# Convolution filters kept as (high, low) pairs instead of two separate rows

## What is computed

```python
x = x + L0(gn(x))     # mixture of 8 experts, top 2: silu(x w1) * (x w3), then w2
x = x + L1(gn(x))     # three causal depthwise convolutions (3, 7, 15 taps), then a 96 -> 32 mix per head
x = x + L2(gn(x))     # the same with other weights
x = x + L3(gn(x))     # the same with other weights
```

## Time and profile before

| | |
|---|---|
| median of three runs | 1167.75 us (1167.03 to 1170.06) |
| the profiled execution | 1165.23 us, span 1163.6 us |
| mean granted TensorE clock | 0.957 |
| TensorE matmuls busy | 1058.7 us, 91% |
| weight loads busy | 881.7 us, 76% (beside matmuls) |
| VectorE, ScalarE, GpSimd busy | 494.9, 318.1, 138.7 us |

### The profile page before, as it was taken

One profiled execution on the slowest core, in us unless ns is written; L12 is line 12 of the kernel. 1 busy time (PEld: TensorE's weight loads), 2 busy tenths in 40 slices (PEclk: granted clock), 3 DMA queues, 4 the chain that ended last, 5 costly groups with the idle time before them and its releaser, 6 DMA issues. The chain is left out here.

```text
span 1163.6 us, 14424 instructions
## 1 busy us (share of the span) xinstructions
PE 1058.7 (91%) x5266; PEld 881.7 (76%) x5267; DVE 494.9 (43%) x677; ACT 318.1 (27%) x433; POOL 138.7 (12%) x170
## 2 busy tenths in 40 slices
PE   5579999999999999999999999357999979999998
PEld 2377887887887887887877878247888967888887
DVE  5744245244245163245362452045424862378011
ACT  2402143243143153143341431112301220122112
POOL 2002121220221221221122211100000000000000
PEclk9769999999999999999999999768999989999999
DMA  9236216415613718316419132293998299688993
GB/s 361 82 116 231 36 28 236 145 27 186 204 26 130 252 27 288 102 27 224 157 28 352 27 128 36 67 265 76 212 185 183 48 219 215 142 173 188 202 208 100
DMA packets 66336, 172.72 MB, mean 148 GB/s; under 512 B 8192, under 2 KB 38016, under 8 KB 57280
## 3 DMA queue, kind: packets, MB, share of 16 engines
q1 hardware_dynamic: 58080, 149.19, 45.1%
q0 software_dynamic: 8080, 23.07, 9.4%
q10 hardware_dynamic: 144, 0.02, 0.0%
HBM read 136.15 MB, written 40.30 MB: 152 GB/s over the span
## 5 line engine op out<-in xcount | busy, mean ns | idle before, releaser
L1345 PE MATMUL head_ps<-split,ring 128*128 128x512 f32 (+1 forms) x630 | 223.9, 355 | 15.6 <-DMA ring<-filters 13.9
L1349 PE MATMUL head_ps<-split,ring 128*128 128x512 f32 (+1 forms) x630 | 218.4, 347 | 0.0
L1346 PE MATMUL head_ps<-split,ring 128*128 128x512 f32 (+1 forms) x630 | 218.2, 346 | 0.0
L1345 PEld LDWEIGHTS head_ps<-split,ring 128*128 128x128 f32 x630 | 121.7, 193 | 32.0 <-DMA ring<-filters 14.5
L1349 PEld LDWEIGHTS head_ps<-split,ring 128*128 128x128 f32 x630 | 121.6, 193 | 15.9 <-DVE split L1163 0.2
L1346 PEld LDWEIGHTS head_ps<-split,ring 128*128 128x128 f32 x630 | 121.9, 194 | 14.8
L860 PE MATMUL y_ps<-w_hi,hT_hi 128*128 128x512 f32 x280 | 115.9, 414 | 1.2 <-ACT hT_hi L526 1.2
L747 DVE TENSOR_TENSOR hidden<-silu,up_ps 128x1024 f32<-128x1024 f32 x35 | 42.7, 1219 | 171.8 <-ACT silu L544 171.8
L860 PE MATMUL y_ps<-w_lo,hT_hi 128*128 128x512 f32 x280 | 112.4, 401 | 0.0
L1172 DVE TENSOR_TENSOR stream<-stream,head_ps 128x512 f32<-128x512 f32 (+1 forms) x63 | 34.1, 557 | 173.2 <-PE head_ps L1349 173.2
L435 POOL DMA_INDIRECT acc<-y_row,put x35 | 76.9, 2197 | 212.7 <-ACT y_row L532 203.5
(11 more groups left out here) (179 smaller groups left out, 1359.3 us busy)
## 6 DMA issues: line engine op xcount, KB each, us to landing
w_raw<-in_w13T SPq DMA_DIRECT2D x32, 1024.0 KB, 10.9
ring<-filters SPq DMA_DIRECT2D x60, 480.0 KB, 10.3
filters<-rows SPq DMA_DIRECT2D x14, 1568.0 KB, 7.6
w_raw<-in_w2T SPq DMA_DIRECT2D x16, 1024.0 KB, 6.3
ring<-filters SPq DMA_DIRECT2D x84, 192.0 KB, 6.1
ring<-filters SPq DMA_DIRECT2D x48, 288.0 KB, 7.1
rows<-in_x SPq DMA_DIRECT2D x4, 1024.0 KB, 7.9
rowed<-acc SPq DMA_DIRECT2D x4, 1024.0 KB, 11.6
```

The costliest lines, as they stand in the source:

```text
L1345: nc.tensor.matmul(place, kernel_hi, x_hi, start=(u == 0 and a == 0), stop=False)
L1346: nc.tensor.matmul(place, kernel_lo, x_hi, start=False, stop=False)
L1349: last = nc.tensor.matmul(place, kernel_hi, x_lo, start=False, stop=(u == len(units) - 1 and a == windows(s) - 1))
```

## The change

The high and the low part of each filter word now stand side by side. `filters` in DRAM has the part as its last dimension. In SBUF the two parts of `filter_sb` alternate word by word, so the clearing on GpSimd (L444), the products (L718), the copy (L516) and the subtraction (L726) write and read every second word; their code is the same, only the view that they go through is another. The store L368 is still one contiguous run for each partition. The ring loads L1008 have the same number, bytes and partitions, but for each unit one run of twice the length instead of two runs. TensorE loads its weight blocks (L1345, L1346, L1349) with a step of two words: the high part begins at the even words, the low part at the odd ones. The number and order of all instructions and all waits stay.

```diff
--- before.py
+++ after.py
@@ -132,7 +132,7 @@
 
 
     acc = nc.dram_tensor("acc", [TOKENS + P, D], f32).ap()
-    filters = nc.dram_tensor("filters", [HD, CHUNKS * P // HD, 2, LAGS], f32).ap()
+    filters = nc.dram_tensor("filters", [HD, CHUNKS * P // HD, LAGS, 2], f32).ap()
     with ExitStack() as ctx:
         def sb(name, shape):
             return ctx.enter_context(nc.sbuf_tensor(name, shape, f32))
@@ -194,7 +194,7 @@
 
         early_w2 = w2_raw[:, :, :].rearrange("p k n -> p (k n)")
         late_rows = rows[:, :, :].rearrange("p i n -> p (i n)")
-        filter_sb = late_rows[:, 0:4 * LAGS].rearrange("p (i s n) -> p i s n", i=2, s=2)
+        filter_sb = late_rows[:, 0:4 * LAGS].rearrange("p (i n s) -> p i s n", i=2, s=2)
         taps_sb = late_rows[:, 4 * LAGS:4 * LAGS + CHUNKS * sum(SCALES)].rearrange("p (c k) -> p c k", c=CHUNKS)
         mix_at = 4 * LAGS + CHUNKS * sum(SCALES)
         mix_sb = late_rows[:, mix_at:mix_at + CHUNKS * 3 * HD].rearrange("p (c s d) -> p c s d", c=CHUNKS, s=3)
@@ -365,8 +365,8 @@
                     load_w2(sp, e, half)
                 for i in range(2):
                     wait_apart(sp, filter_ok, e * 2 + (i - 1), sp_passed)
-                    sp.dma_start(filters[:, bass.ds(e * 8 + (4 * i - 8), P // HD)].rearrange("r a s n -> r a (s n)"),
-                                 filter_sb[:, i].rearrange("p s n -> p (s n)")).then_inc(filters_out, 16)
+                    sp.dma_start(filters[:, bass.ds(e * 8 + (4 * i - 8), P // HD)].rearrange("r a n s -> r a (n s)"),
+                                 late_rows[:, 2 * LAGS * i:2 * LAGS * (i + 1)]).then_inc(filters_out, 16)
 
         @block.gpsimd
         def _(pool):
@@ -898,7 +898,7 @@
     ALU, ACT, AX = mybir.AluOpType, mybir.ActivationFunctionType, mybir.AxisListType
     acc_rows = acc[0:TOKENS, :].rearrange("(b p q) n -> b p q n", p=P, q=QUARTERS)
     out_rows = out.rearrange("b (p q) h w -> b p q (h w)", q=QUARTERS)
-    filter_rows = filters.rearrange("r j s n -> r (j s) n")
+    filter_rows = filters.rearrange("r j n s -> r j (n s)")
 
     with ExitStack() as ctx:
         def sb(name, shape, dt=f32):
@@ -1005,8 +1005,8 @@
                     at, width = (RING_AT[i] + taken) * 2 * P, windows(s) * P
                     for q in range(QUARTERS):
                         begin = SCALE_AT[s] + (QUARTERS - 1 - q) * HD
-                        sp.dma_start(ring[HD * q:HD * (q + 1), at:at + 2 * n * width].bitcast(f32).rearrange("r (a n) -> r a n", n=width),
-                                     filter_rows[:, 2 * (l * GROUPS + j0):2 * (l * GROUPS + j0 + n), begin:begin + width]).then_inc(ring_in[h], 16)
+                        sp.dma_start(ring[HD * q:HD * (q + 1), at:at + 2 * n * width].bitcast(f32).rearrange("r (a n) -> r a n", n=2 * width),
+                                     filter_rows[:, l * GROUPS + j0:l * GROUPS + j0 + n, 2 * begin:2 * (begin + width)]).then_inc(ring_in[h], 16)
 
             load_rows(0)
             load_rows(1)
@@ -1337,8 +1337,7 @@
                         between(n, u)
                     piece = l * len(PIECES) + PIECE_OF[j, pair] + 1
                     for a in range(windows(s)):
-                        kernel_hi, kernel_lo = (ring[:, (2 * at + part * windows(s) + a) * P:(2 * at + part * windows(s) + a + 1) * P]
-                                                for part in range(2))
+                        kernel_hi, kernel_lo = (ring[:, 2 * (at + a) * P + part:2 * (at + a + 1) * P:2] for part in range(2))
                         x_hi, x_lo = (split[:, j, part, bs.start:bs.stop, LEAD - a:LEAD - a + P] for part in range(2))
                         if a == 0:
                             pe.wait_ge(high_ok, piece)
```

## The result

Six executions each on one chip: the changed kernel 1175.3 us (median, 1173.6 to 1176.7), the kernel before 1168.7 us (1167.0 to 1170.1). The ratio is 1.0049, 95% interval 1.0036 to 1.0061, which is 4.2 to 7.1 us: slower, by a little more than a measurement here can tell from nothing. The forecast was no change.

A forecast was written before the change was run, and what follows sets the result against it. TensorE, busy 91% of the span, was taken as the bound, with head matmuls paced by their column stream. Weights, ring, filter work and memset at 0 us each kept the median at 1167.5 us, own range 1164.5 to 1170.5, wide 1157 to 1192.

The forecast's parts named there:

- The weight loads: Head matmuls' 128x128 weight loads, read with a step of two: claimed to stay hidden behind the column stream, 0 us, at most 96 us.
- the room of 0.119 us: Head matmuls with 256 columns: time between successive matmuls, in which a load of at most 0.113 us was claimed to hide.
- The third rival: Head matmuls: weight loads become slower than the stream of 256 columns, 66 us (1233 us) to 96 us (1263 us); chance 0.11.
- The cachelines rule: SBUF accesses in the filter work: two accesses in a 16-byte line suffice, so a step of two words is free, 0 us.
- The filter work: Expert part, L718, L516 and L726 with 8 bytes between words: claimed unchanged, 0 us, bound 24 us.
- the first rival: Expert part: VectorE and ScalarE pay up to 0.62 ns more per element, up to 24 us, 1192 us; chance 0.17.
- The rule of adjacent pairs: VectorE's L718 and L726: full rate needs adjacent word pairs; single words cost up to 2.50 instead of 1.05 ns, 40 us.
- The ring: Filter transfers from DRAM to the ring: doubled descriptors claimed to bring no speed, 0 us, rate staying 219 to 223 GB/s.
- The second rival: Ring transfers get faster, 326 instead of 219 GB/s, and stalls shrink: 10.9 us gained, 1157 us; chance 0.16.
- The clearing: POOL's L444 at a step of two: up to 3.9 us longer, covered by 7.56 us of idle time, 0 us.
- The sum: Whole kernel: weights, ring, filter work and memset at 0 us each, median staying at 1167.5 us; chance 0.56.
- the wide range: Whole kernel: 1157 to 1192 us, holding the forecast and the first two rivals to their bounds, without slower weight loads.

## Why the prediction was wrong, by its own steps

**The weight loads, 0 us: wrong, and this is the step that failed.** It measured 4.0 us alone (2.6 to 5.4). The reasoning was "the pace is the stream of columns and no weight load shows in it: a load that cost time of its own would add the same to both". The earlier trace rows could not carry that: 7 steps read at a resolution of 10 ns leave 1.4 ns open, and the question was one of 2 ns in 1890 places. Nor are the two paces of the kernel before in the ratio of the columns: over the long stretches twice 119.5 is 239.0 ns, 5 ns more than 234.1, so some fixed time was there already (whose it is, no run shows). What appeared with the step is just the thing the sentence excluded, a time that adds the same to both. The large part of the step held: the room of 0.119 us, the load of at most 0.113 us from the earlier trace rows, and its doubling as the upper end. The doubling is there at step four, 0.235 us, but not at step two. That step four cost 91 us in all where the bound said 96 is near by chance: 900 x 0.115 = 104 us and 990 x 0.006 = 6 us, less 9 us of stalls for the ring that shrank beside it (4.9 instead of 13.9 us), leave 10 us that these terms don't explain. The third rival (66 to 96 us) was therefore wrong here by one doubling of the step. Its 0.119 us point did decide: steps of three and four passed it.

The cachelines rule that the prediction cited (the Trainium skill, SBUF — State Buffer, Door 1: The DMA port swizzle), two accesses in a line of 16 bytes suffice, agrees with the large term: with one word per line (step four) a load takes 234.7 ns, with two (step two) no more than 121.6. The same note calls four fp32 words a free stride; the row for a step of four (234.7 instead of 119.5 ns) contradicts that, and the measurement decides. Neither statement has the 2 ns.

**The filter work, 0 us: VectorE right, ScalarE wrong by a little.** L726 1789 against 1788 ns, L718 unchanged. L516 took 0.15 us more, 0.1 ns per element, which is the first rival's mechanism on one of its three lines at the very point (0.09 ns) from which it was to matter. It came to 1.5 us (0.2 to 2.8), on a bound of 24. The rule of adjacent pairs (the Trainium skill, Vector Engine (DVE) Microarchitecture Reference, 5.2 Measured stream behaviour on trn2), by which VectorE would have lost an estimated 40 us, is not borne out at a step of two words (1789 against 1788 ns).

**The ring, 0 us: right.** The rate stayed at 218 and 228 GB/s with packets twice as long; alone the long packets cost 0.7 us (-0.7 to 2.0). The second rival, faster transfers, is gone. The stall of 8.4 us that the profile after shows looked like a cost of the change and goes with an instruction fetch that also strikes kernels with short packets. That long packets make it likelier is not excluded (three of four profiles against two of ten) and was not tried further.

**The clearing, 0 us: right.** 0.5 us more on GpSimd, inside the 7.56 us of the earlier trace rows.

**The sum.** 4.0 + 1.5 + 0.7 = 6.2 us from the parts, 5.1 and 5.7 us by the ratios of the whole. Two small terms, and a third that can't be told from nothing, each taken as nothing, made a difference that can be measured. The predicted time of 1167.5 us was 7.8 us low, and its own range ended at 1170.5. That the wide range, up to 1192 us, held the result is luck: its upper end was drawn for the conversions, and most of the difference came from the weight loads, which it left out.

## What to carry to other kernels

A price of 2 ns is not small when 1890 instructions on the path pay it: to call a pace unchanged or a load hidden, take a stretch of 100 or more instructions, and multiply the resolution of the reading by the count before writing 0. Weights in SBUF may lie two words apart for 2 ns a load, but three or four words cost 56 and 115 ns where the matmuls behind them have only 256 columns. And the waits that a change would lengthen are worth looking at for themselves: moving the products took all seven away and gave 27 us, nearly five times what the change cost.

## What was not expected of the hardware

- A load of 128 weights per partition costs 1.83 ns for each 16 bytes touched at steps three and four (175.2 and 234.7 ns), and apart from that 2.0 to 10.8 ns at steps two to eight that not even 512 columns hide.
- ScalarE's copy with a step of two words, in and out, takes 1.66 instead of 1.51 us for 1568 elements; VectorE's subtraction of that size takes the same.
- A stall of 2.4 us can cost TensorE more than itself: after four of the seven such stalls the granted clock was 0.5 to 0.6 for 3.5 us, and removing 17.3 us of such stalls gave 27 us.
- Where one instruction fetch of 0.02 MB fell into the burst of ring loads, TensorE's first wait for them was 3 us longer, in one execution of a kernel and not in another.
